# Banded attention in a chained model kernel: from one batch at a time to a step that covers three

## The reference

```python
def local_attention(q, k, v):            # 8 heads of 64, window 64
    ...
    bk, bv = (look_around(bk), look_around(bv))   # a block of keys and the one before it
    sim = jnp.einsum('bhwid,bhwjd->bhwij', bq, bk)
    mask = (i < j) | (i > j + WINDOW) | (j == -1)
    sim = jnp.where(mask, -jnp.finfo(sim.dtype).max, sim)
    attn = jax.nn.softmax(sim, axis=-1)
    out = jnp.einsum('bhwij,bhwjd->bhwid', attn, bv)

def _layer(x, wqkv, qs, ksc, wo, ...):
    h = shift_token(x)
    q, k, v = jnp.split(h @ wqkv, 3, axis=-1)     # then to heads
    q, k = rotary_xpos(l2norm(q) * qs, l2norm(k) * ksc)
    o = local_attention(q, k, v)
    x = x + o @ wo
    ...                                           # gated feed-forward, a part of its own
```

## Time and profile before

| | us |
|---|---|
| median of 3 runs | 5345.99 (5333.31 to 5357.66) |
| profiled run, its device time | 5364.76 |
| profiled run, span from first to last instruction | 5362.6 |
| TensorE busy (rows of matmuls) | 4220.5, 79% |
| VectorE busy | 3846.1, 72% |
| GpSimd busy | 2812.2, 52% |
| ScalarE busy | 2401.0, 45% |
| mean granted TensorE clock | 0.869 |

### The profile page before, as it was taken

How to read it: one execution, slowest core, us unless ns; L and a number is a source line. 1 busy time by engine, 2 the same in 40 slices (tenths; PEclk the granted TensorE clock), 3 DMA queues, 4 the chain that set the end, 5 groups by cost and what they waited for, 6 DMA issues and landing times. The chain is left out here.

```text
span 5362.6 us, 75658 instructions
## 1 busy us (share of the span) xinstructions
PE 4220.5 (79%) x19773; PEld 2678.0 (50%) x19773; DVE 3846.1 (72%) x6816; ACT 2401.0 (45%) x4956; POOL 2812.2 (52%) x2705
## 2 busy tenths in 40 slices
PE   5999999999577667658778875588888867888884
PEld 4777777777466456547335553233333323333332
DVE  5766766666465356456227776699999969999995
ACT  3545545454133233223224443266666625666661
POOL 2555555555333143133002223089999908999991
PEclk8989988888677767678879997699999978999997
DMA  1000000000000000000000000000000000000000
GB/s 47 8 8 8 8 8 8 9 7 8 14 0 0 19 0 0 7 4 0 22 16 1 1 1 14 8 0 0 0 0 0 0 7 0 0 0 0 0 0 12
DMA packets 89933, 33.17 MB, mean 6 GB/s; under 512 B 77888, under 2 KB 85968, under 8 KB 88784
## 3 DMA queue, kind: packets, MB, share of 16 engines
q1 hardware_dynamic: 89680, 30.15, 2.4%
HBM read 24.86 MB, written 5.24 MB: 6 GB/s over the span
## 5 line engine op out<-in xcount | busy, mean ns | idle before, releaser
L2878 POOL TENSOR_TENSOR dBx<-dtx,b_row 128x1024 f32<-128x1024 f32 x512 | 1219.8, 2383 | 3.9 <-ACT b_row L2844 3.9
L2912 DVE TENSOR_TENSOR_SCAN h<-banks,dBx 128x1024 f32<-128x1024 f32 x512 | 1168.5, 2283 | 18.5 <-ACT banks L2838 18.5
L2796 PE MATMUL banks<-hc,ident 128*128 128x512 f32 x2048 | 964.4, 593 | 0.0
L2838 ACT ACTIVATE banks<-dt,A 128x510 f32<-128x510 f32 x1024 | 661.6, 682 | 3.6 <-DVE h L2912 3.6
L2844 ACT ACTIVATE b_row<-banks 128x512 f32<-128x512 f32 x512 | 305.9, 598 | 574.2 <-PE banks L2780 574.2
L2796 PEld LDWEIGHTS banks<-hc,ident 128*128 128x128 f32 x2048 | 388.6, 190 | 272.5 <-issue 247.1
L2920 DVE TENSOR_TENSOR hc<-h,banks 128x768 f32<-128x768 f32 x512 | 478.5, 935 | 9.9 <-ACT c_row L2849 6.6
L2887 POOL TENSOR_TENSOR hc<-h,c_row 128x256 f32<-128x256 f32 x512 | 376.7, 736 | 55.1 <-ACT c_row L2849 28.7
L2780 PE MATMUL banks<-bc_lo,selectors 128*128 128x512 bf16 x1024 | 391.3, 382 | 0.0
L2779 PE MATMUL banks<-bc_hm_c,selectors 128*128 128x512 bf16 x512 | 197.3, 385 | 186.8 <-DVE hc L2920 186.8
L801 POOL TENSOR_TENSOR weighted<-probs,f 128x1024 f32<-128x1024 f32 x64 | 121.8, 1903 | 359.0 <-DVE f L844 359.0
(11 more groups left out here) (411 smaller groups left out, 9319.3 us busy)
## 6 DMA issues: line engine op xcount, KB each, us to landing
delta_blocks<-A_turned SPq DMA_DIRECT2D x256, 8.0 KB, 1.5
inv_turned<-delta_blocks SPq DMA_DIRECT2D x256, 8.0 KB, 1.7
blocks<-delta_blocks SPq DMA_DIRECT2D x32, 64.0 KB, 2.1
delta_blocks<-blocks_inv SPq DMA_DIRECT2D x32, 64.0 KB, 1.9
wh<-in_l1f_wh SPq DMA_DIRECT2D x1, 2048.0 KB, 8.3
wqkv<-in_l0f_wqkv SPq DMA_DIRECT2D x2, 768.0 KB, 4.1
residual<-in_x SPq DMA_DIRECT2D x1, 1024.0 KB, 4.7
wv<-in_l0a_wv SPq DMA_DIRECT2D x1, 1024.0 KB, 7.2
```

The costliest lines, as they stand in the source:

```text
L2796: i = nc.tensor.matmul(k.bank[e], k.ident[:], hc[:, s, e, :], start=False, stop=False)
L2838: i = nc.scalar.activation(a3[:, :, 1:], d3[:, :, 1:], ACT.Exp, scale=mem["A"][:, e, bass.ds(n, 1)])
L2878: nc.gpsimd.tensor_tensor(dBx[:, s % NS], dtx[:, :, bass.ds(c * SCH, SCH)], across(bsb[:, s % NS, :], SE), ALU.mult).then_inc(q["dbx_ready ...
L2912: v.tensor_tensor_scan(flat(h[:, s % NS]), flat(k.banks[:, at:at + SE, :]), flat(dBx[:, s]), 0.0, ALU.mult, ALU.add).then_inc(q["scanned"], 1)
```

## The change

The order of work on all engines is rewritten; the arithmetic is the same. A step now covers three batches: x0 = b gets steps 1 and 2 and its norms, x1 = b - 1 gets the normalising, the rotation, the scores, the exponentials, the turned probabilities and the heads of unit 0, and x2 = b - 2 gets the heads of unit 1, the output turning, the final projection and the addition. A helper `batches` writes two filling steps, a hardware loop of six and two emptying steps, so there are ten steps for eight batches.

The turned probabilities of both units go to banks 4 to 6, which they share with the projection. The output turning is done per unit, four transposes each, into bank 7, and the final projection goes to bank 7 too. The semaphores' conditions follow from that: the projection waits for the copies of the turned probabilities, the second unit's heads for the first output copy, and so on. The wait for `y_added` moves from the turning of q and k to the heads of unit 0.

```diff
-        TB = (4, 0)
+        TB = 4
...
+        def batches(eng, step):
+            step(0, None, None)
+            step(1, 0, None)
+            with eng.Fori(2, B) as b:
+                step(b, b - 1, b - 2)
+            step(None, B - 1, B - 2)
+            step(None, None, B - 1)
...
                 def heads_of(b, u):
                     pe.wait_ge(q["pt_act"], (b * NU + u) * 2 + 2)
                     pe.wait_ge(q["pt_dve"], b * NU + u + 1)
-                    pe.wait_ge(q["heads_out"], b * NU + u + 1)
+                    if u == 0:
+                        pe.wait_ge(q["v_moved"], b + 1)
+                        after(pe, "y_added", b)
+                    else:
+                        pe.wait_ge(q["ot_ready"], b * NU + 1)
```

The new order of TensorE, each line under `if x… is not None`:

```diff
+                def step(x0, x1, x2):
+                        turn_out(x2, 0)
+                        heads_of(x2, 1)
+                        project(x0, 0)
+                        turn_qk(x1)
+                        project(x0, 1)
+                        score(x1, 0)
+                        turn_out(x2, 1)
+                        score(x1, 1)
+                        last_projection(x2)
+                        turn_probs(x0, x1, 0)
+                        heads_of(x1, 0)
+                        turn_probs(x0, x1, 1)
```

Of ScalarE:

```diff
+                def step(x0, x1, x2):
+                        move_v(x1)
+                        read_out(x0, 0)
+                        copy_turned(x1, 0)
+                        copy_turned(x1, 2)
+                        read_out(x0, 1)
+                        copy_out(x2, 1)
+                        exponentials(x1, 0)
+                        copy_probs(x1, 0)
+                        exponentials(x1, 1)
+                        copy_probs(x1, 1)
+                        copy_out(x1, 0)
```

Of VectorE:

```diff
+                def step(x0, x1, x2):
+                        load_x(x0)
+                        normalised(x1)
+                        out(x2, 0)
+                        copy_probs(x2, 1)
+                        rotated(x1)
+                        out(x2, 1)
+                        copy_turned(x1)
+                        norms(x0, 0)
+                        banded(x1, 0)
+                        maxima(x1, 0)
+                        norms(x0, 1)
+                        banded(x1, 1)
+                        add_y(x2)
+                        maxima(x1, 1)
+                        copy_probs(x1, 0)
```

More of the change, by code:

```diff
@@ L1352, in _, with move_v @@
+                batches(pe, step)
             @block.scalar
             def _(act):
+                def move_v(b):
+                    act.wait_ge(q["read_out"], b * TPB + TPB)
+                    after(act, "heads", b * NU)
+                    nc.scalar.activation(v[:], raw[:, :, 2, :], ACT.Copy).then_inc(q["v_moved"], 1)
                 def read_out(b, t):
+                    if t == 0:
+                        after(act, "v_moved", b)
+                        after(act, "normed", b * TPB)
@@ L1391, in _, with copy_turned @@
-                for t in range(TPB):
-                    read_out(0, t)
-                batch(0, 1)
-                with act.Fori(1, B - 1) as b:
-                    batch(b, b + 1)
-                batch(B - 1, None)
+                def copy_turned(b, n):
+                    act.wait_ge(q["turned"], b * 4 + n + 1)
+                    nc.scalar.activation(qkT[:, n // 2, :, 0:P], k.bank[n].rearrange("p (c t) -> p c t", c=CB),
+                                         ACT.Copy).then_inc(q["t_act"], 1)
@@ new lines, in exponentials @@
+                def exponentials(b, u):
+                    act.wait_ge(q["maxed"], b * NU + u + 1)
+                    for h in range(HG):
+                        for t in range(TPB):
+                            src = S[:, u, h, 0:W0] if t == 0 else S[:, u, h, W0:]
+                            dst = E[:, u, h, 0:W0] if t == 0 else E[:, u, h, W0 + T - W1:]
+                            i = nc.scalar.activation(dst, src, ACT.Exp, scale=8.0, bias=mx[:, u, h, t:t + 1],
+                                                     accum_out=rs[:, u, h, t:t + 1])
+                    i.then_inc(q["exped"], 1)
@@ L1399, in _ @@
+                batches(act, step)
             @block.gpsimd
@@ L1416, in _ @@
                     g.tensor_tensor(flat, flat, half[:], ALU.pow).then_inc(q["norm_ready"], 1)
+                    after(pool, "turned", b * 4)
                     for t in range(TPB):
@@ L1464, in rotated, with copy_turned @@
                     i.then_inc(q["rotated"], 1)
+                def copy_turned(b):
+                    for n in (1, 3):
+                        dve.wait_ge(q["turned"], b * 4 + n + 1)
+                        vv.tensor_copy(qkT[:, n // 2, :, P:T], k.bank[n].rearrange("p (c t) -> p c t", c=CB)).then_inc(q["t_dve"], 1)
                 def banded(b, u):
@@ L1489, in out, with add_y @@
                     i.then_inc(q["heads_out"], 1)
-                def batch(b, behind):
-                    if behind is not None:
-                        load_x(behind)
-                    for n in (1, 3):
-                        dve.wait_ge(q["turned"], b * 4 + n + 1)
-                        vv.tensor_copy(qkT[:, n // 2, :, P:T], k.bank[n].rearrange("p (c t) -> p c t", c=CB)).then_inc(q["t_dve"], 1)
-                    for u in range(NU):
-                        banded(b, u)
-                        if behind is not None:
-                            norms(behind, u)
-                    for u in range(NU):
-                        copy_turned(b, u)
-                    out(b, 0)
-                    if behind is not None:
-                        normalised(behind)
-                    out(b, 1)
-                    if behind is not None:
-                        rotated(behind)
+                def add_y(b):
@@ L1524, in window_ffn_layer @@
+                batches(dve, step)
 def window_ffn_layer(k, l):
```

181 lines of the change are left out of this document (88 added, 93 removed).

## The result

The changed kernel takes 5220.24 us (median of 4 runs, 5210.06 to 5220.66) against 5347.58 for the kernel before (4 runs, 5333.31 to 5357.66): a ratio of 0.976, 95% interval 0.973 to 0.979, some 127 us saved where 86 were forecast. The profiled run took 5219.92 us, with a span of 5217.8 us.

What follows compares the result with a forecast made beforehand. A ring of waits, no engine being full, was taken to bound banded attention. 49.8 + 6 x 34 + 50.6 = 304.4 us a layer, 608.8 for both, 86 less than 695.2, gave 5260 us; range 5190 to 5305.

Steps and rivals of the forecast that it cites:

- the ring: In banded attention, a cycle of waits between engines, none full, sets the period: 37.9 to 41.4 us a batch before.
- the walk: Summed timing of one new step from its first projection: 29 us at full clock, 33.7 with four TensorE pieces slow.
- The steps of 32 to 36 us: Mixed-clock outcome for the new loop's steps, chance 0.57; 34 us was taken.
- fill, up to the first whole step: Start of each pass: 32.4 to the first q/k turning, 3.5 for it slow, 13.85 to step end; 49.8 us.
- six steps: The whole steps of the loop in each layer, 34 us each.
- drain: Emptying steps of each layer: about 28 without projection and norms, 22.6 for the last; 50.6 us.
- The likeliest case: Mixed clock in the new step: walked as 33.7 us, taken as 34; chance 0.57.
- second turning, output turning, second heads and the first projection are slow: TensorE pieces of the step assumed at 1.2 GHz, giving a step of 33.7 us.
- full clock nearly throughout: Rival: TensorE at 2.4 GHz, steps of 29 us, 158 us saved, 5188 us; chance 0.25.
- the rule cited for the rotation: Skill's rule: VectorE operations with two SBUF inputs and GpSimd ones reading SBUF take turns on shared ports for whole instructions.
- No effect: Rival: the ring only changes members, steps of 38 to 40 us, 0 to 25 us saved, some 5335; chance 0.05.
- Slower: Rival: clock stays at 1.2 GHz through the dense part too, steps of 43.5 us, 5389 us; chance 0.05.

Runs made afterwards that it cites:

- the fills: Changed kernel plus four unused 512-column matmuls a step in TensorE's waits; 5191.18 us, ratio 0.972 to the kernel before.
- the output chain moved away: Kernel with the fills, plus the first output turning and its copy moved behind the second projection; 5186.29 us, ratio 0.970.
- one bank less for VectorE: Kernel with the fills, but the third bank of each unit's turned probabilities copied by ScalarE instead of VectorE; 5189.08 us, ratio 0.972.
- old banks: Changed kernel with unit 1's turned probabilities in banks 0 to 2 again, and the waits that follow; 5229.9 us, ratio 0.979.
- fill in one place: Changed kernel plus only the two unused matmuls before the first unit's turned probabilities; 5211.99 us, ratio 0.977.
- cost added with and without fills: One unused VectorE reduction inside the rotation: added to the changed kernel 5223.86 us, to the kernel with the fills 5216.43 us; both ratio 0.978.

## Why the prediction was right, and where its sizes were off

The mechanism and the forecast's case held: the ring is the one walked but for one link, the clock is mixed, and the time lies in the range. The link is GpSimd's power, which the walk had hidden. The steps of 32 to 36 us, to which most of the chance was given, did not come: 30.8 lies between them and the 29 of full clock, and the range held because it spans both. The saving was larger than forecast, and each term can be set beside its measurement.

| term, us a layer | forecast | measured, first pass |
|---|---|---|
| fill, up to the first whole step | 49.8 | 52.7 (1424.29 to 1477.03) |
| six steps | 6 x 34 = 204 | 184.1, 30.7 each |
| drain | 50.6 | 46.2 |
| sum | 304.4 | 283.0 |

The fill was 2.9 too short and the drain 4.4 too long, so these two partly made up for each other.

**The step is the term that was mis-sized.** The likeliest case was walked as 33.7 and set at 34. Three things make it 30.8. First, heads at half clock throughout were put at 5.4 us, and they took 4.7 (1606.96 to 1611.66), because the clock fell only after the first of them: 0.7. Second, the first projection was put at 5.4 up to the q/k turning, and was 3.94 (1611.66 to 1615.60): 1.5. Third, from the q/k turning to the next second heads, outside the low clock, I counted 22.95 us (16.4 to the normalising, 6.55 from there), and the step has 15.85 and 6.28: 0.8. Here VectorE's step began 0.85 sooner than summed (14.75 against 15.6), mostly because the loop's branch, counted at 0.6, shows no gap at all between the copy at 1629.75 and the load at 1630.35; but 0.52 of what VectorE gained went into the wait for the power. Together 3.0, and 33.75, which the walk comes to unrounded, less 3.0 is the 30.8 of the trace. So the step that failed is "second turning, output turning, second heads and the first projection are slow": I took the half-clock stretch as whole pieces, some 15 us of a step, where the windows show 6 to 7 us that begin and end within pieces. The projection in particular has the clock come back in its own middle, as 4.10, between 2.7 and 5.5, tells; the 5.46 of the earlier trace rows stands behind a long wait and was the wrong row for it. Rows in between lay in the trace of before too (4.89 in the earlier trace rows, and 3.59 at 1986.05), and I should have taken one.

**The clock's place in the forecast.** I named 0.70 to 0.78 for a step of 34 and above 0.9 for 29; it is 0.79 and 0.82 for 30.8, and 1.00 for 28.2. The rival "full clock nearly throughout" was therefore half right: its step of 29 exists (28.2), and the fills reach it, but the changed kernel doesn't. The rule of the Trainium skill that was weighed there (TensorE: Matmul & The Clock Gate, "Why this matters for your kernels": keep TensorE busy, without long gaps) gave that rival. The longest idle time of TensorE in the step shown is 1.94 us, and yet the clock falls, so the rule as I read it doesn't hold here; but in its direction it is right, since work put into these short waits brought the clock back.

**Rotation against TensorE.** At full clock the rotation was to be last by 1.0 us. It is: TensorE waits 0.60 for it in the kernel with fills and 1.40 with the output chain moved away. Its price was put at 7.2 us and it took 7.0 (1605.98 to 1612.99), the first half 4.32 against 4.5, between the 3.18 of the earlier trace rows and the 5.79 of the earlier trace rows. The load of x, which by the rule cited for the rotation would wait for the power, did not: it lies at 1599.58, inside the power's 1595.22 to 1600.65, and took 0.28 us (0.29 in the earlier trace rows). For these two operations that rule doesn't hold here. At the mixed clock it was to be 2.1 us ahead of TensorE (31.6 against 33.7), and VectorE's wait for the turning was named as its longest; it is, with 2.74 where 5 were named for a step of 34. That an extra 1.22 us there left most steps at 30.8 shows the slack.

**What was put at nothing.** The text said that the prediction is wrong if VectorE waits for GpSimd's power, and VectorE does wait for it, 0.4 to 0.5 us in most steps. The power came when summed (15.8 us behind the q/k turning, 15.9 summed); VectorE was there 1.1 us sooner than summed. The price of that is at most half a microsecond a step, but it puts the power on the ring, where the walk had it hidden by 0.5 us: work taken from VectorE ahead of it gains nothing, as the kernel with one bank less for VectorE showed. The shared banks 4 to 6 cost and bring nothing (565.1 us with either set). Output turning at full clock (0.66 for four, 0.55 forecast up to the next start) and the final projection (2.05, 2.1 forecast) were near; the first output turning came 1.1 us behind the scaling (1604.43 to 1605.53), as said.

**Fill and drain.** The fill is 2.9 longer. Its q/k turning came 34.1 us after the first projection, where I took the 32.4 of the old order, and the second projection behind it took 3.84 instead of 2.7. The drain is 4.4 shorter: its last additions lie 20.8 us apart where my terms give some 25 (22.6, and 3 from an addition to the end of its step), since I put all of the last step at half clock. In the timeline, turning and heads run at either level there:

```profile
1687.81 1.53 PE L1326 MATMUL banks<-ident,probs 128*128 128x128 f32 x12 [1.73 <-ACT probs L1411]
...
1692.93 2.81 PE L1326 MATMUL banks<-ident,probs 128*128 128x128 f32 x12
...
1703.37 3.50 PE L1357 MATMUL banks<-wo,heads_out_featmajor 128*128 128x128 f32 x16 [0.69 <-ACT heads_out_featmajor L1423]
```

**The other rivals.** "No effect" fell with the steps: the hand-overs between the new members cost 1.31 and 0.78 us around the output turning, where that rival put some 4 us more at each. "Slower" would have needed half clock in the dense part, and the second projection and the scores ran at full clock (1.00 from 1616 to 1628). For scores at the low clock the prediction had no row and took 2.9 us a unit; in the emptying step they took 2.57 (1679.03 to 1681.60). That the sum of the passes saved 130 us and the medians differ by 127 agrees; the profiled runs differ by 145 because the one of before started its first pass late.

**What stays open.** Why the clock falls where it does, within heads that follow each other without a gap, no run here settles, nor why the same kernel has steps of 30.0, 30.8 and 31.7 us; which of the thin places matters most is open too, since filling the first alone restored only two of ten steps.

## What to carry over

When several chains of one item stand behind each other in a loop while every engine is under 80% busy, look for the ring, and spread one item's chain over several turns: here it took 38 to 41 us of ring down to 31, and filling the clock's gaps alone in the old order left it at 37.6. Price TensorE's pieces in a mixed stretch by rows of the same kind of neighbourhood, not at one of the two levels throughout. Where waits of TensorE are short and its clock is low, unused matmuls in those waits are a cheap test of how much the clock costs (2.6 us of 30.8), and a version to keep (32 us with the later output turning); once it runs at full clock, a delay can lose more than its own length (2.6 us for 1.22 here). And when a step comes out as the sum of two stretches, as 15.86 and 12.37 us here, shorten what lies on them: the two copies taken off VectorE lay on neither.

## What the runs showed of the hardware

A change of 1.2 us on VectorE cost 0, 1.2 or 2.6 us a step, and a chain shortened by 1.6 us gained 0.4. The lengths of steps recur: 30.8 us in five kernels (changed, old banks, fill in one place, cost added with and without fills), 28.2 in three, 37.5 or 37.6 in two that share only the old order. In the new order they recur because the stretch from q/k turning to normalising is 15.85 us in nearly every step of these kernels, and the other one is 12.37 at full clock, with the rotation last, or 14.90 to 14.96 with part of it at the low clock. That the latter comes out nearly the same each time is measured and not explained: second heads and first projection together took 8.64 us in the changed kernel (4.70 and 3.94) and 8.66 in the one with fills and the added cost (3.95 and 4.71), where the low clock began and ended later.

The clock was 0.50 in 2 us windows in which TensorE's rows were busy for 2.00 us, in the heads of before and after alike (and 1608 to 1610 above), and at 1.00 under a step with 25.28 of 28.00 us busy. The busy share in the records doesn't tell the clock.

The same eight operations of the rotation's first half took 2.76 us where 4.3 us lay between them and the normalising (at 1485.57 in the changed kernel), 4.32 behind 1.73, 4.92 behind 1.13, 4.94 behind 1.11 and 5.79 directly behind it, where GpSimd's product with the cosine table runs. In the three cases between, gap and duration add up to 6.05 us: what was moved out from ahead of the rotation came back in full.
